# A second place for turned probabilities in a recurrence that carries causal attention beside it

## The reference

```python
# causal attention and experts (per 128 rows this depends on earlier rows only)
q = l2norm(q) * q_scale;  k = l2norm(k) * k_scale
logits = einsum('bhid,bhjd->bhij', q, k) * 10, masked above the diagonal
attn = softmax(logits);  out = einsum('bhij,bhjd->bhid', attn, v) ... @ Wo
gate = softmax(layernorm(out) @ gate_w + gate_b)
moe = sum_e gate_e * (gelu(h @ w1_e + b1_e) @ w2_e + b2_e)
...
# attention-GRU, 512 steps, each needs the state of the one before
score = enc . (h @ W);  attn = softmax(score);  context = attn . enc
z = sigmoid(xz + hz);  r = sigmoid(xr + hr);  cand = tanh(xh + r * hh)
h = z * h + (1 - z) * cand
```

## Time and profile before

| | us |
|---|---|
| three runs | 3392.69, 3431.45, 3389.45 |
| median | 3392.69 |
| the profiled execution's own time | 3399.51 |
| its span | 3397.6 |
| PE busy | 2864.2 (84%) |
| ACT busy | 1736.5 (51%) |
| ACT's wait at L1869 for L1666 | 150.2 in 61 places |

### The profile page before, as it was taken

The page is one execution under the profiler, slowest core; times in us unless marked ns, Lnnn a source line. Parts: engine busy times, 40 slices in busy tenths (PEclk is TensorE's granted clock), DMA queues, the critical chain, the costliest instruction groups (busy, mean ns, idle before and its releaser), DMA issues. The chain is left out here.

```text
span 3397.6 us, 132510 instructions
## 1 busy us (share of the span) xinstructions
PE 2864.2 (84%) x54702; PEld 1897.3 (56%) x54702; DVE 2216.0 (65%) x8486; ACT 1736.5 (51%) x5855; POOL 883.5 (26%) x1882
## 2 busy tenths in 40 slices
PE   5999999776987888898888899899989877777678
PEld 3666666653554454465454566566656544444478
DVE  4666666754426656677566677777768766666665
ACT  3666666433633444475555476666657433333222
POOL 0000000210002444254555344655535200000000
PEclk8999999987888878899899999999999999999879
DMA  4000000000010000010000000000000000000001
GB/s 130 4 5 7 5 4 4 1 10 9 16 51 9 9 9 27 3 40 4 9 9 27 4 28 16 7 10 10 25 10 28 4 3 3 3 4 3 2 32 32
DMA packets 35640, 52.45 MB, mean 15 GB/s; under 512 B 5406, under 2 KB 22760, under 8 KB 34920
## 3 DMA queue, kind: packets, MB, share of 16 engines
q1 hardware_dynamic: 34280, 41.54, 3.9%
q0 software_dynamic: 768, 2.52, 0.3%
HBM read 40.48 MB, written 3.57 MB: 13 GB/s over the span
## 5 line engine op out<-in xcount | busy, mean ns | idle before, releaser
L2010 POOL TENSOR_TENSOR gru_terms<-gru_states,gru_signs 128x8 f32<-128x8 f32 x512 | 103.5, 202 | 1573.7 <-DVE gru_states L2216 1245.0
L1931 ACT ACTIVATE gru_p<-gru_ps_sg,gru_negmax 128x78 f32<-128x78 f32 x512 | 166.9, 326 | 379.1 <-DVE gru_negmax L2185 374.0
L1774 PE MATMUL gru_ps_sg<-score_w,gru_states 128*4 128x78 f32 x4096 | 168.3, 237 | 194.7 <-DVE gru_states L2216 194.5
L1935 ACT ACTIVATE gru_th_r<-gru_pre_r 128x32 f32<-128x32 f32 x512 | 118.4, 231 | 398.6 <-DVE gru_pre_r L2196 398.6
L1572 PE MATMUL gru_ps_sg<-ctx_gate_w,gru_p_t 128*4 128x64 f32 x12288 | 281.1, 228 | 0.0
L342 ACT ACTIVATE self_probs<-self_sc,self_negmax 128x512 f32<-128x512 f32 x256 | 174.2, 684 | 166.2 <-DVE self_negmax L396 166.2
L1987 POOL TENSOR_SCALAR bg_probs<-bg_probs,bg_arsum 128x256 f32<-128x256 f32 (+2 forms) x192 | 240.5, 1253 | 19.0
L2205 DVE TENSOR_TENSOR_SCAN gru_c_in<-gru_th_r,gru_own 128x64 f32<-128x64 f32 x512 | 152.1, 297 | 123.3 <-ACT gru_th_r L1935 123.3
L1778 PE MATMUL gru_ps_own<-late,gru_states 128*4 128x128 f32 x4096 | 216.9, 285 | 0.0
L2185 DVE TENSOR_REDUCE gru_negmax<-gru_ps_sg 128x1 f32<-128x78 f32 x512 | 121.9, 238 | 141.0 <-PE gru_ps_sg L1774 135.6
L2196 DVE SCALAR_TENSOR_TENSOR gru_pre_r<-gru_ps_sg,gru_rtotal,gru_own 128x32 f32<-128x32 f32 x512 | 127.1, 248 | 129.1 <-PE gru_ps_sg L1572 118.9
(11 more groups left out here) (386 smaller groups left out, 7426.8 us busy)
## 6 DMA issues: line engine op xcount, KB each, us to landing
bg_w<-in_moe_w SPq DMA_DIRECT2D x48, 256.0 KB, 3.0
bg_wa<-in_wqkv SPq DMA_DIRECT2D x24, 192.0 KB, 2.3
moe_w<-in_moe_w SPq DMA_DIRECT2D x16, 256.0 KB, 2.9
picked_w_sb<-in_ec_w SPq DMA_DIRECT2D x16, 256.0 KB, 2.9
cross_scratch<-ctab_raw SPq DMA_DIRECT2D x16, 154.0 KB
late<-in_late SPq DMA_DIRECT2D x1, 2397.5 KB
cross_outs<-cross_scratch POOLq DMA_DIRECT2D x4, 576.0 KB, 6.2
self_w_sb<-in_wqkv SPq DMA_DIRECT2D x8, 192.0 KB, 2.3
```

The source lines that it names most:

```text
L1774: last = pe.matmul(ps_s[32 * b:32 * b + B, 0:CTX + 1], state(t), score_w[:, b, 0:CTX + 1], start=False, stop=True, tile_position=(0, 32 * ...
L1931: act.activation(p[:, 0:CTX + 1], ps_s[:, 0:CTX + 1], ACT.Exp, bias=negmax[:, 0:1], accum_out=total[:, 0:1])\
```

## The change

Units of groups at pace 2 alternate between two places: even m in `hid`, odd m in the first two thirds of `u`. The copy then waits for the values of the units up to m - 2, not m - 1. One wait is added: the first chunk of a group's experts, which writes `u` again, waits for the values of all the group's units. Group 3 stays as it was. No engine gets or loses an instruction other than waits.

```diff
-        probs_t = hid
...
+        def turned_probs(g, m):
+            return u[:, 0:2, :] if PACE[g] == 2 and m % 2 else hid[:]
...
             def values(g, n, m):
...
-                        last = pe.matmul(bk_out[half, 0:P], v, probs_t[:, j, kt * P:(kt + 1) * P], start=kt == 0, stop=kt == g,
+                        last = pe.matmul(bk_out[half, 0:P], v, turned_probs(g, m)[:, j, kt * P:(kt + 1) * P], start=kt == 0, stop=kt == g,
...
             def unit_input(g, n, m):
                 act.wait_ge(s_up, m + 1)
                 wait_positive(act, s_hid, m - 2)
+                if n == 0:
+                    act.wait_ge(s_val, g * U)
...
             def take_turned(g, n, m, j):
                 act.wait_ge(s_apt, 2 * m + j + 1)
-                wait_positive(act, s_val, m)
+                wait_positive(act, s_val, m - 1 if PACE[g] == 2 else m)
                 if n < 2:
                     wait_positive(act, s_down, 2 * (g - 1) * C)
-                act.activation(probs_t[:, j, 0:(g + 1) * P], bk_turn[:, 0:(g + 1) * P], ACT.Copy).then_inc(s_apte, 1)
+                act.activation(turned_probs(g, m)[:, j, 0:(g + 1) * P], bk_turn[:, 0:(g + 1) * P], ACT.Copy).then_inc(s_apte, 1)
```

## The result

The changed kernel takes 3238.99 us (median of 4 runs, 3238.18 to 3240.48). The kernel before, run again beside it, took 3412.07 (3389.45 to 3435.76). The ratio is 0.949 with a 95% interval of 0.941 to 0.958. Two later runs of the kernel before (3439.62 and 3443.18 us) are more than 1.5% slower than its fastest and are left out of every comparison here. The profiled executions are 3397.6 and 3236.4 us long, a difference of 161.2 us.

What follows compares the result with a forecast made beforehand. A 512-step recurrence was taken to stand still where ScalarE's copy waits for values matmuls. 108 us of stall plus up to 49 of clock made 157, less 1.8 and 4 kept back: 151 saved, 3245 us, range 3230 to 3296.

Steps and rivals of the forecast that it cites:

- The wait is the cost: ScalarE's copy of turned probabilities waits 150.2 us in 61 places for the previous unit's values matmuls, holding up the tanh.
- PE is late next: Even steps of groups 1 and 2: PE's projection, values and mask limit the gain to 1.75 and 1.86 us; 108 us with tails.
- The clock recovers: Both groups' stretches: without the stall TensorE runs at full clock, granted clock 0.97 or more.
- Rival A: Attention groups 1 and 2: the clock keeps falling on small gaps, only 108 us saved, 3285 to 3291 us; chance 0.17.
- Rival C: Steps 8 to 62 and 122 to 177: TensorE stays at the lower level, 123 us more, some 3515; chance 0.04.
- rival B: The copy: another condition ending at the same time holds it; 3393 us in full, 3318 in mild form; chance 0.06.
- The size of the clock term: Time at TensorE's lower level: 30.5 us in group 1's stretch, 18.6 in group 2's, 49 us at most.
- run 49: Not a run's label: 49 is the clock term's upper bound in us, 30.5 + 18.6, for groups 1 and 2.
- The tails: Six steps without a projection, tanh held by 1.34 us in the one shown; about 1.2 us each, 7 us.
- What I kept back: 1.8 us for two late weight loads and 4 us for clock falling for other reasons, taken off the saving.
- The division of a pair into even and odd steps: After the change, even steps of about 3.9 us (group 1) and 4.2 us (group 2), odd ones 3.76.
- The second place, the added wait, POOL's and DVE's work: Probabilities in u, the wait at an expert stage's first chunk, and POOL and DVE, which keep their work: priced at nothing.

Runs made afterwards that it cites:

- the dose on PE: Changed kernel plus four 128x256 bf16 fill matmuls on PE after the mask in each of 62 even steps: 3272.16 us, against 3241.76.
- the filled stall: Kernel before, wait kept, plus eight 128x256 bf16 fill matmuls on PE after the mask in each stalled step: 3348.9 us, ratio 0.983.

## Why the prediction was right, step by step

I said 3245, with a range of 3230 to 3296; it is 3239.

- *The wait is the cost: the copy waits for the values matmuls.* Shown: gone in the changed kernel, back when the wait alone is put back.
- *PE is late next, so 1.75 and 1.86 us a step.* The tanh alone would have given 2.18 in group 2 and 1.84 in group 1, for which the prediction doesn't work it out (in the step of the earlier trace rows the tanh starts at 1115.00, pre_r is ready at 1113.13, and 0.03 us between them is the least). Shown by size, above all in group 2, where the two differ more: 1.76 and 1.91 with the clock up; and by the dose on PE, which came through whole. My 108 us for this part were 107.
- *The clock recovers.* That it went to 1.00 is in the changed kernel's rows; that the stall had held it down is shown by the kernel with the filled stall. Rival A, a clock left at 0.82 and 0.92, did not come true. The section of the Trainium skill's "TensorE: Matmul & The Clock Gate" that I had weighed for it speaks of brief and frequent idling and gives no length for it. The kernel before, whose PE paused 1.7 to 1.8 us in every second step, agrees with it (0.72 to 0.96); the changed kernel, whose PE pauses 30 times for 0.2 to 0.37 us in group 1's stretch and twice, for 0.22 and 0.67 us, in group 2's, stays at 1.00. Rival C, the low clock throughout, has its denial in the same rows, and rival B, that another condition holds the copy, in the single 0.5 us wait that is left.
- *The size of the clock term* was right in sum for the execution that I read, and in part by luck. Against the filled stall, group 1's stretch gave 294.8 - 264.9 = 29.9 us (I said 30.5), group 2's 293.8 - 280.3 = 13.5 (I said 18.6, since I took one quiet pair for all 28 and the first pairs are longer), and the tails, where I had put nothing, 3.5 and 2.5: 49.4 in all. For a typical run 49 is too small. The same kernel's runs differ by 49 us, and their time goes with the clock: 3387.93 us at a mean granted clock of 0.941, 3436.66 at 0.924. The median run has 71 us in it. My saving (151) was too low against a median of 3412 to 3426: it was 173 to 185. My absolute time was not hurt, and that is luck too: the two times that I began from, 3399.5 and 3392.7, are both of the quicker kind. From a median of 3426 the same 151 us would have led to 3275, still inside the range.
- *The tails.* I gave them 7 us; they gave 7.1 + 6.5. My 1.2 us a step was the stall alone, and as that it was right: against the filled stall the tails give 3.5 + 4.0. The clock recovered there too (0.73 and 0.85 before, 0.94 and 1.00 after).
- *What I kept back.* Against 28 x 7.69 = 215.3 and 28 x 7.97 = 223.2, the stretches took 215.7 and 226.8. The 4 us kept for other falls of the clock were not used for that. Group 2 is 3.6 us over because its first three pairs take 9.44, 8.37 and 9.06 us in place of 7.97, with the stretch's clock at 1.00; what makes them long was not looked into. The two late weight loads were not late any more: PE has no wait for them in the changed kernel's first stretch.
- *The division of a pair into even and odd steps failed.* I said 3.9 and 4.2 us for even steps and 3.76 for odd ones, from state write to state write. Group 1's average 3.86 and 3.84. In group 2 even steps average 111.5 / 28 = 3.98 and odd ones 115.3 / 28 = 4.12. The pair's sum is right to 0.02 us in group 1 and 0.13 in group 2. The state is now written early in the even step, by the tanh's chain, and PE's lateness appears between this state and the next scores, so in the odd step. The dose on PE shows the same: all of its 13.8 us in group 1 came in odd steps (108.4 to 122.3 us), though the fills belong to the even ones. I had priced by the scores' start and announced by the state's.
- *The second place, the added wait, POOL's and DVE's work* cost nothing, as put.

What stays open is why the old group 1 falls to the lower level more often than the old group 2 (23 to 28 falls against 7 to 11), and why group 1's time there differs so much from run to run (89 to 184 us). No run here takes that apart.

## What to carry to other kernels

A wait for a buffer (write after read) on one engine may be paid twice: once by the work behind it in that engine's order, and once by TensorE, which idles meanwhile and can fall to the lower clock for the work after it. The two can be told apart by filling the idle time with matmuls that nobody reads. Before one prices a shortened wait, one follows the order of every engine to the next event: in group 2 it was 1.9 us of 2.2, because PE's own work ended 0.3 us later. And a kernel whose clock falls in some of its steps has no single time: it takes several runs, each with its granted clock, and a profile is one of them.

## What the runs showed of the hardware

- A stall of about 2.5 us on ScalarE in every second step, in which PE idles 1.7 to 1.8 us, went with a granted clock of anything between 0.72 and 0.96 over such a stretch. With PE's idle time cut to 0.8 us by fills it was 0.99 to 1.00.
- 102 of the 103 falls of the clock in such stretches came 0.7 to 3.8 us after a pause of PE of over 1.2 us began. Set against the filled stall, 106, 89 and 184 us at the lower level cost group 1's stretch 30, 22 and 66 us.
- The three kernels in which group 1 still stalls with PE idle vary by 37 to 51 us from run to run; the others by 2 to 8, also the one in which group 2 alone still stalls (4).
- A matmul that waits for another engine with nothing ahead of it on PE started 0.147 us after the event; with a short fill matmul running up to the event, mostly 0.05 to 0.10. That is some 0.07 us for a matmul that nobody reads.
